# A cross-network kernel on one core: slabs 0 and 1 take their field rows from SBUF, early loads reordered, small operands merged

## What is computed

```
def _cin_layer(x0, x, kernel):
    W = kernel.reshape(m, h_prev, kernel.shape[1])
    return jnp.einsum('bmd,bhd,mho->bod', x0, x, W)
x = x0
finals = []
for k in (k1, k2, k3):
    x = _cin_layer(x0, x, k)
    finals.append(jnp.sum(x, axis=-1))
logit = jnp.concatenate(finals, axis=-1) @ kf
```

## Time and profile before

| | us |
|---|---|
| median of 3 runs | 309.11 |
| profiled execution | 308.59 |
| its span | 306.8 |
| PE busy | 295.5 (96%) |
| POOL busy | 228.2 (74%) |
| DVE busy | 194.0 (63%) |
| ACT busy | 180.3 (59%) |

### The profile page before, as it was taken

The page is one execution under the profiler, slowest core; times in us unless marked ns, Lnnn a source line. Parts: engine busy times, 40 slices in busy tenths (PEclk is TensorE's granted clock), DMA queues, the critical chain, the costliest instruction groups (busy, mean ns, idle before and its releaser), DMA issues.

```text
span 306.8 us, 8019 instructions
## 1 busy us (share of the span) xinstructions
PE 295.5 (96%) x3190; PEld 86.5 (28%) x3190; DVE 194.0 (63%) x213; ACT 180.3 (59%) x197; POOL 228.2 (74%) x132
## 2 busy tenths in 40 slices
PE   7697999999999999999999999999999999999995
PEld 2441222222222222222222222222222222222231
DVE  0736746577775666677765666677665666777632
ACT  1547467376775747567764747567664747677511
POOL 7476589878796968969796977979696987979700
PEclk9779799999999999999999999999999999999999
DMA  7999999999999979797996979697996979520100
GB/s 248 381 351 349 340 421 307 414 317 409 362 355 353 303 293 295 271 318 295 326 345 275 299 275 297 268 342 309 319 322 272 292 270 307 235 68 2 36 0 3
DMA packets 17371, 86.25 MB, mean 281 GB/s; under 512 B 2636, under 2 KB 3020, under 8 KB 8652
## 3 DMA queue, kind: packets, MB, share of 16 engines
q1 hardware_dynamic: 15352, 78.04, 69.1%
q10 hardware_dynamic: 2004, 8.00, 11.0%
HBM read 86.02 MB, written 0.01 MB: 280 GB/s over the span
## 4 chain that ended last, share of the span: by engine, by line
PE 86%; DMA 7%; SPq 3%; POOL 1%; issue 1%; DVE 1%; ACT 0%; ACTq 0%; POOLq 0%
PE acc L540 69%; PE acc L548 10%; PE rot L526 7%; DMA v<-v_rows 7%; SPq L231 1%; POOL prod L374 1%; SPq L223 0%; POOL low L380 0%; POOL split L384 0%; ACTq L215 0%; SPq L236 0%; SPq L239 0%; SPq L238 0%; DVE xy L470 0%; DVE sums L472 0%
## 5 line engine op out<-in xcount | busy, mean ns | idle before, releaser
L540 PE MATMUL acc<-prod,w 128*32 128x512 f32 x2048 | 229.2, 599 | 0.0
L374 POOL TENSOR_TENSOR prod<-u,v 128x1024 f32<-128x1024 f32 x64 | 152.6, 2385 | 21.7 <-PE acc L540 15.0
L540 PEld LDWEIGHTS acc<-prod,w 128*32 128x32 f32 x2048 | 63.7, 111 | 150.0 <-issue 139.1
L282 ACT ACTIVATE prod<-rot 128x1024 f32<-128x1024 f32 x64 | 65.3, 1020 | 33.2 <-PE rot L526 26.2
L464 DVE TENSOR_TENSOR prod<-rot,u 128x1024 f32<-128x1024 f32 x64 | 77.8, 1216 | 2.5 <-PE rot L526 1.5
L470 DVE TENSOR_TENSOR xy<-acc,ysb 128x512 f32<-128x512 f32 x32 | 22.1, 692 | 90.4 <-ACT ysb L299 90.4
L464 DVE TENSOR_TENSOR prod<-rot,v 128x1024 f32<-128x1024 f32 x64 | 77.8, 1215 | 0.0
L299 ACT ACTIVATE ysb<-acc,kf 128x512 f32<-128x512 f32 x32 | 22.0, 687 | 78.3 <-PE acc L548 48.5
L380 POOL TENSOR_TENSOR low<-xc,split 128x512 f32<-128x512 f32 x31 | 36.3, 1171 | 33.9 <-ACT split L290 33.9
L286 ACT ACTIVATE feat<-u 96x2048 f32<-96x2048 f32 x32 | 60.9, 1904 | 0.6 <-DMA v<-v_rows 0.6
L384 POOL TENSOR_TENSOR split<-low,split 128x512 bf16<-128x512 f32 x31 | 36.1, 1163 | 2.2 <-ACT split L294 1.5
(11 more groups left out here) (40 smaller groups left out, 24.4 us busy)
## 6 DMA issues: line engine op xcount, KB each, us to landing
u<-u_rows SPq DMA_DIRECT2D x30, 1024.0 KB, 4.9
v<-v_rows SPq DMA_DIRECT2D x30, 1024.0 KB, 8.7
xc<-x_chunks SPq DMA_DIRECT2D x32, 256.0 KB, 10.2
feat<-u_rows ACTq DMA_DIRECT2D x30, 256.0 KB, 7.7
u<-u_rows SPq DMA_DIRECT2D x4, 512.0 KB, 9.9
v<-v_rows SPq DMA_DIRECT2D x4, 512.0 KB, 12.4
u<-k3p SPq DMA_DIRECT2D x2, 512.0 KB, 4.9
v<-k2t SPq DMA_DIRECT2D x1, 512.0 KB, 6.6
```

What stands on the lines that cost most here:

```text
L282: nc.scalar.activation(prod[p][:, WW, pair(n)], rot[:, pair(n)], ACT.Square).then_inc(squares_ready, 1)
L374: nc.gpsimd.tensor_tensor(prod[p][:, UV, pair(half)], us[n][:, pair(half)], vs[n][:, pair(half)], ALU.mult).then_inc(uv_ready, 2)
L540: mm = nc.tensor.matmul(acc[p][h][quad(c), :], w[:, t, h * G:(h + 1) * G], prod[p][:, t, chunk(c)], start=(t == first), stop=(first is Non ...
```

## The change

* The squares of the fields of slabs 0 and 1 are followed on ACT by a copy of the fields, 32 partitions by 2048 columns, from U (partitions 96 to 127) to `feat`, and `feat_ready` is given by the copy. The two `place_fields` of SyncE go, and the waits for `feat_in` count one transfer less.
* SyncE's queue: the chunk of x of slab 2 goes ahead of slab 1's U and V, that of slab 3 ahead of slab 2's.
* `kz`, the last column of `vk`, the bias and `pick` come in one array of 258 columns. DVE copies vk's column and casts `picks` from it at the start of its program, and `v_ready` counts 2.
* TensorE: three matmuls of zeros between T and rotation 0, and the fixes for h = 0 ahead of T's tables.

```
             load_xc(1, 1)
             load_halves(0, 0)
+            load_xc(2, 2)
             load_halves(1, 1)
-            place_fields(sp, 0, 0)
             load_halves(1, 0)
-            load_xc(2, 2)
+            load_xc(3, 3)
             load(2, 2)
-            place_fields(sp, 1, 1)
-            load_xc(3, 3)
...
-                nc.scalar.activation(feat[p][FEATS, :], us[n][FEATS, :], ACT.Square).then_inc(feat_ready, 1)
+                squares = nc.scalar.activation(feat[p][FEATS, :], us[n][FEATS, :], ACT.Square)
+                if isinstance(s, int) and s < 2:
+
+                    nc.scalar.copy(feat[p][quad(3), :], us[n][quad(3), :]).then_inc(feat_ready, 1)
+                else:
+                    squares.then_inc(feat_ready, 1)
...
             act.dma_start(kzs[:], kz).then_inc(kz_in, 16)
-            act.dma_start(pick32[:], pick).then_inc(pick_in, 16)
-            act.dma_start(vk[:, WRAP:], kf[M:M + H1, :]).then_inc(kf2_in, 16)
-            act.dma_start(kf1[:], bass.AP(tensor=kf.tensor, offset=0, ap=[[0, CHUNKS], [1, M], [1, 1]])
-                          ).then_inc(kf1_in, 16)
...
+            dve.wait_ge(kz_in, 16)
+            nc.vector.tensor_copy(vk[:, WRAP:], kzs[:, KF2]).then_inc(v_ready, 1)
+            nc.vector.tensor_copy(picks[:], kzs[:, PICK]).then_inc(picks_ready, 1)
             dve.wait_ge(vt_ready, 1)
...
             split_low(0)
-            dve.wait_ge(pick_in, 16)
-            nc.vector.tensor_copy(picks[:], pick32[:]).then_inc(picks_ready, 1)
             split_last(0)
...
-            pe.wait_ge(v_ready, 1)
-            pe.wait_ge(kf2_in, 16)
+            pe.wait_ge(v_ready, 2)
...
             mm.then_inc(t_ready, 1)
+            keep_clock_up(acc[1][0], 3)
             pe.wait_ge(picks_ready, 1)
             pe.wait_ge(first_split, 1)
             rotate(0)
+            pe.wait_ge(w_ready[0], 1)
+            pe.wait_ge(fix_in, 16)
+            fixes_of(0)
             for n in range(2):
                 pe.wait_ge(tt_ready[n], 2)
             tables_of_t()
-            pe.wait_ge(w_ready[0], 1)
-            pe.wait_ge(fix_in, 16)
-            fixes_of(0)
             pe.wait_ge(w_ready[1], 1)
             fixes_of(1)
```

More of the change, by code:

```diff
@@ L41 @@
 FEATS = slice(0, (Q - 1) * M)
+KZ, KF2, KF1, PICK = slice(0, 4 * M), slice(4 * M, 4 * M + 1), slice(4 * M + 1, 4 * M + 2), slice(4 * M + 2, 8 * M + 2)
 def index(pair, q, i):
@@ L71, in selections, with small @@
             np.concatenate([fix.reshape(P, 4 * P), fold.reshape(P, M)], axis=1))
[L74 to L78, removed]
+def small(kf, pick):
+    kz = np.zeros((P, KZ.stop + 2 + P), np.float32)
+    kz[0:H2, M] = kz[H2:, M + 1] = kf[M + H1:, 0]
+    kz[:, 2 * M:KZ.stop] = np.tile(np.eye(M, dtype=np.float32), (Q, 2))
+    kz[:, KF2] = kf[M:M + H1]
+    kz[:, KF1] = np.tile(kf[0:M], (Q, 1))
+    kz[:, PICK] = pick
     return kz
@@ L85, in wait, with cin_kernel @@
         engine.wait_ge(semaphore, value)
-def cin_kernel(nc, u_rows, v_rows, x_chunks, k1g, k2t, k3p, kz, kf, pick, fixes, out):
+def cin_kernel(nc, u_rows, v_rows, x_chunks, k1g, k2t, k3p, kz, fixes, out):
     with ExitStack() as ctx:
@@ L113, in cin_kernel @@
         k2s = vs[NBUF - 1][:, 0:M * G]
-        kzs = sb("kzs", [P, 4 * M])
+        kzs = sb("kzs", [P, PICK.stop])
         tt = prod[1][:, UW:, :].rearrange("p t n -> p (t n)")[:, 0:(M + WRAP) * 2 * M]
@@ L124, in cin_kernel @@
         wf = sb("wf", [P, G])
-        kf1 = sb("kf1", [P, 1])
-        pick32 = sb("pick32", [P, P])
+        kf1 = kzs[:, KF1]
         picks = sb("picks", [P, P], BF16)
@@ L141, in cin_kernel @@
         rest_ps = acc[1][1][2 * M:, 2 * G:3 * G]
-        k2_in, kf2_in, kf1_in = (sem(n) for n in ("k2_in", "kf2_in", "kf1_in"))
-        kz_in, k3_in = sem("kz_in"), [sem(f"k3_in{n}") for n in range(K3_PARTS)]
-        pick_in, fix_in, k1_in = sem("pick_in"), sem("fix_in"), sem("k1_in")
+        k2_in, kz_in, k3_in = sem("k2_in"), sem("kz_in"), [sem(f"k3_in{n}") for n in range(K3_PARTS)]
+        fix_in, k1_in = sem("fix_in"), sem("k1_in")
         first_in = [[sem(f"first_in{s}{half}") for half in range(2)] for s in range(2)]
@@ L298, in take_y @@
                 wait(act, xy_ready, s - 1)
-                nc.scalar.activation(ysb[p][:], acc[p][1][:], ACT.Identity, bias=kf1[:]).then_inc(y_ready, 1)
+                nc.scalar.activation(ysb[p][:], acc[p][1][:], ACT.Identity, bias=kf1).then_inc(y_ready, 1)
             act.dma_start(kzs[:], kz).then_inc(kz_in, 16)
-            act.dma_start(pick32[:], pick).then_inc(pick_in, 16)
-            act.dma_start(vk[:, WRAP:], kf[M:M + H1, :]).then_inc(kf2_in, 16)
-            act.dma_start(kf1[:], bass.AP(tensor=kf.tensor, offset=0, ap=[[0, CHUNKS], [1, M], [1, 1]])
-                          ).then_inc(kf1_in, 16)
             act.wait_ge(xc_in[0], 16)
@@ L324, in _ @@
             square_fields(0, 0, 0)
-            act.wait_ge(kf1_in, 16)
+            act.wait_ge(kz_in, 16)
             def step(it, n):
@@ L635, in _ @@
             pe.wait_ge(feat_ready, 1)
-            pe.wait_ge(feat_in[0], 16)
             for h in range(2):
@@ L658, in step @@
                 pe.wait_ge(feat_ready, s + 1)
-                pe.wait_ge(feat_in[p], 32 * it + 16 * (n // 2 + 1))
+                wait(pe, feat_in[p], 32 * it + 16 * (n // 2))
                 more = not isinstance(s, int) or s + 1 < SLABS
@@ L663, in step @@
                     pe.wait_ge(feat_ready, s + 2)
-                    pe.wait_ge(feat_in[1 - p], 32 * it + 16 * ((n + 1) // 2 + 1))
+                    pe.wait_ge(feat_in[1 - p], 32 * it + 16 * ((n + 1) // 2))
                 contract(s, 1, p, tiles[-1:], UV).then_inc(taken, 1)
@@ L705 @@
                                     ).reshape(P, M // 2, H1),
-        "kz": last_of(np.asarray(L0_rec_kf)[M + H1:, 0]),
-        "kf": np.ascontiguousarray(L0_rec_kf),
-        "pick": pick,
+        "kz": small(np.asarray(L0_rec_kf), pick),
         "fixes": fixes,
```

## The result

| | before | after |
|---|---|---|
| median of 20 runs each, us | 309.23 | 310.94 |
| lowest and highest, us | 307.96 to 311.28 | 308.04 to 312.61 |
| profiled execution, us | 308.59 | 310.81 |
| its span, us | 306.8 | 308.9 |

The ratio is 1.0050, 95% interval 1.0026 to 1.0074 (1.0055 by the two medians): the change made the kernel slower by half a per cent, where I had forecast no measurable change.

The account below looks back on a forecast made before the run. TensorE's unbroken work from 31.20 us was the bound; only its start, T2, could move. Gains in loads and TensorE's set-up, spent by the +1.57 us copy, left -0.2 us: 309.11 - 0.2 = 308.9 us, range 307.8 to 310.6 us.

Parts of the forecast that it names:

- The bound: TensorE is busy 271.49 of 271.80 us from 31.20 us; this steady part was to cost the same afterwards.
- T2: Start of slab 2's rotation on TensorE, where the steady part begins; 31.20 us before, forecast 31.0 us.
- The loads: DMA queues: without the field loads, V's first half of slab 1 lands at 23.86 instead of 25.06 us.
- The dips: DMA rate falls from 418 to 224 and 223 GB/s, ascribed to the field loads, costing 1.04 us.
- the top part's start: ACT begins the top part of x of slab 2; 25.84 us before, forecast 23.95 to 24.2 us.
- both conditions lay at 25.1 us: Slab loads and rotation 1 with ACT's squares of W release ACT's top part together; gaining on one alone gives nothing.
- my sum: Top part at 24.07 plus 6.93 us to T2 gives 31.0 us, -0.2 us; 308.4 us on the profiled execution.
- rotation 1 ... **0.9 to 1.3 us earlier: TensorE's rotation of slab 1 begins at 21.8 to 22.2 us instead of 23.09 us.
- After it the first slab stays at 1.2 GHz as before: Behind T2 the first slab costs 1.39 + 8.08 us as before, though TensorE's pause grows from 2.7 to about 4 us.
- The copy: ACT's copy of slab 1's fields takes 1.80 us in the chain from top part to T2: 6.93 instead of 5.36, +1.57 us.
- TensorE's first 23 us: Set-up: fixes wait until 13.3 us, first contraction begins at 17.95 to 18.45 us and takes 3.5 instead of 5.24 us.
- The wait for the fixes costs the clock: Rival: TensorE idles until 13.3 us, clock stays at 1.2 GHz, T2 32.5 us, +1.3, 310.4 us; chance 0.25.

Follow-up runs that it names:

- e6: Changed kernel with 14 matmuls of zeros on TensorE in the pause ahead of rotation 2; ratio to the kernel before 1.0003.
- e7: Changed kernel without the three matmuls of zeros between T and rotation 0, fixes still ahead of the tables; ratio to the kernel before 1.0105.
- g1: Kernel before with 10 matmuls of zeros added on TensorE ahead of rotation 2; ratio to the kernel before 0.9981.
- e2: Changed kernel with TensorE's part undone: no idle matmuls before rotation 0, fixes behind T's tables; ratio to the kernel before 1.0126.
- e3: Kernel before with only ACT's copies of the fields and SyncE's new load order; ratio to the kernel before 1.0034.
- h1: The kernel of e2 measured again, TensorE's part of the changed kernel undone; ratio to the kernel before 1.0091.
- e1: Changed kernel with slab 1's copy of the fields moved on ACT behind slab 2's middle part; ratio to the kernel before 0.9949, again 0.9942.
- e8: Changed kernel with fields loaded by SyncE, no ACT copies, and 13 matmuls of zeros ahead of rotation 2; ratio to the kernel before 0.9952.
- h5: Second measurement of e1's kernel with 8 matmuls of zeros added ahead of rotation 2; ratio to the kernel before 0.9937.
- g3: Changed kernel with slab 0's fields copied by ACT, slab 1's loaded by SyncE behind slab 2's U and V; ratio to the kernel before 0.9957.
- e4: Changed kernel with fields of slabs 0 and 1 loaded by SyncE, no ACT copies; ratio to the kernel before 0.9906, again 0.9989.

## Why the prediction was wrong

* **The bound** was right: the steady part, where TensorE works without a break, is not touched, and in the profiles all is decided by T2 and by the clock just behind it.
* **The loads** were right in kind. The dips were the fields' and went. V's first half of slab 1 was issued at 8.94 us and landed 13.9 us later, at 22.84 us, 1 us better than my 23.86. It brought nothing, as rotation 1 set the top part's start. One reading was wrong: "both conditions lay at 25.1 us" passes over x of slab 2, which my own row names as what released the top part. It was issued behind V and landed later still, at 9.55 + 16.1 = 25.65 us:

```profile
9.55 0.44 SPq L223 DMA_DIRECT2D xc<-x_chunks  x1
...
xc<-x_chunks SPq DMA_DIRECT2D x1, 256.0 KB, 16.1
```

  After the change, V's first half of slab 1:

```profile
8.94 0.43 SPq L235 DMA_DIRECT2D v<-v_rows  x1
...
v<-v_rows SPq DMA_DIRECT2D x1, 512.0 KB, 13.9
```

* **The steps that failed.** On the profiled execution my sum gave 308.4 us, and it took 310.81. Three terms make up the 2.4 us. The first is "rotation 1 ... **0.9 to 1.3 us earlier**": it came 0.15 us later, 1.2 us off. The second is "After it the first slab stays at 1.2 GHz as before", "because TensorE's pause ahead of it grows from 2.7 to about 4 us", as if the longer pause were free: from rotation 2 to 3 it was 12.10 us in place of 11.28, 0.8 us. The third is the copy.
* **The copy** was mis-sized, "+1.57 us": it measured 7.33 - 5.36 = 1.97 us. I had let the copy overlap its neighbours by 0.1 us like the squares, and had the middle part follow in 0.90 us; it took 1.90, 1.92 and 1.05. It was priced too low by 0.4 us, twice the net gain of 0.2 us that I forecast.
* **TensorE's first 23 us.** Contraction from 17.95 to 18.45 us at the full clock and rotation 1 at 21.8 to 22.2 us came true in e6 and e7, the same program to that point but for three matmuls in e7 (18.23 and 18.06, 21.97 and 21.80 us; T2 at 31.30 and 31.12 us, my 31.0). In the changed kernel's profiled execution the set-up ran at the low clock and all this was 1.2 us later. I took the early part of one execution of before as given.
* **The price of the longer pause** alone would not have taken the time out of my range: with T2 where I put it, e7's profiled execution took 309.31 us. Nor is it a fixed 0.8 us, as the table above shows (11.06 to 12.43 us behind 3.90 us).
* **The coupling.** Before, T2 was held by the loads, V's and behind it x of slab 2. So a late rotation 1 was hidden (23.09 us) and an early one brought nothing (21.70 in g1, T2 31.51). Afterwards both are out of the way, and T2 is rotation 1 plus 9.31 to 9.33 us in the profiles of e2, e3, e6, e7, h1 and the changed kernel. What the clock does in the set-up now goes to T2 unhidden. I had noted that the times of both conditions were alike, but not that the change takes away the cover.
* **The rivals.** "The wait for the fixes costs the clock" put T2 at 32.5 us; it was 32.56, but by another way: in the changed kernel's profiled execution there is no such wait, and the contraction ran at full speed. Elsewhere the wait did not decide: behind waits of 1.11 to 1.28 us in e1, e6 and e7 the contraction ran at the full clock, behind 0.80 and 0.76 us in e8 and h5 it took 5.30 us, with rotation 1 at 23.02 and 23.33 us. The range ended at 310.6 us, below the 310.94 measured, because I had no rival that puts the clock behind T2 on top of a late T2.
* **What stays open.** Eight of the 20 executions of the changed kernel took 311.95 to 312.61 us at a mean granted clock of 0.976 to 0.982; the profiled one had 0.989. No profile shows where the clock was low in those eight, so the three terms account for the profiled execution and not for the whole median.

## What to carry to other kernels

A transfer replaced by an engine's work must be priced at the place in that engine's queue: here 1.9 us cost 2 us between two links of a chain and nothing one position behind the last of them (7.33 and 5.39 us, 5.36 before). When a change shortens one of two nearly equal conditions, ask what the longer one had been hiding. And price the pause ahead of a burst of matmuls together with its effect on the clock, as a range: behind pauses of 1.8 to 2.7 us a burst of 9.64 us took 9.64 or 11.28, behind 3.6 to 5.7 us it took 11.06 to 12.49.

The version to keep is e1's with the 8 matmuls of zeros: slab 1's copy behind slab 2's middle part, 0.9947 and 0.9937, and 0.9959 and 0.9939 by the medians of all executions. Without the zeros it is 0.9949 and 0.9942, but 0.9946 and 0.9989 by those medians.

## What I had not expected of the hardware

Executions of the same program differ by over 4 us (308.04 to 312.61 in 20 runs), and the mean granted clock goes with it: 0.994 in those of 308.04 and 308.07 us, 0.976 to 0.982 in the eight above 311.9. The first four idle matmuls between k3's halves take 1.89 us in some profiles (after, g3) and 1.04 us in others (before, e4), and rotation 1 comes at 21.31 us in e4 and at 24.60 in g3. Comparing two profiled executions therefore needs both the set-up's durations and the clock behind T2, or a difference of this size says nothing of the change.

While a transfer into 32 partitions is under way, all queues together move about 225 GB/s in place of 418. The changed kernel shows it by losing both dips and e4 by bringing one back (229 GB/s).
